# Reordering the end of the edge sweep in a graph-network and mixture-of-experts kernel

## The reference

```python
# x (3125, 256), 53125 edges (src, dst, type), sorted by dst, 8 relations, 16 experts, hidden 512
h_all = jnp.einsum('ni,roi->rno', layernorm(x), weight)       # 8 relations
msgs = h_all[edge_types, src]
x = x + jax.ops.segment_sum(msgs, dst, num_segments=3125) + bias
xn = layernorm(x)
probs = softmax(xn @ gate_w + gate_b)
top_probs, top_idx = jax.lax.top_k(probs, 2)                  # then normalised to sum 1
hidden = silu(xn @ w1[e]) * (xn @ w2[e])                      # for each chosen expert e
x = x + sum over the two experts of top_prob * (hidden @ w3[e])
```

## Time and profile before

| | |
|---|---|
| median of 3 runs | 988.91 us (986.33 to 989.62) |
| the profiled execution | 995.36 us |
| its span, first to last instruction | 993.7 us |
| its mean granted TensorE clock | 0.886 |
| busy: TensorE, VectorE, ScalarE, POOL | 759.2, 509.3, 262.6, 664.6 us |

### The profile page before, as it was taken

The page is one execution under the profiler, slowest core; times in us unless marked ns, Lnnn a source line. Parts: engine busy times, 40 slices in busy tenths (PEclk is TensorE's granted clock), DMA queues, the critical chain, the costliest instruction groups (busy, mean ns, idle before and its releaser), DMA issues.

```text
span 993.7 us, 18212 instructions
## 1 busy us (share of the span) xinstructions
PE 759.2 (76%) x4527; PEld 637.0 (64%) x4528; DVE 509.3 (51%) x1473; ACT 262.6 (26%) x397; POOL 664.6 (67%) x621
## 2 busy tenths in 40 slices
PE   0456797877888788788787884356998999998981
PEld 0334686765767566676666674245887888887871
DVE  6776444546444545544544746847443343443475
ACT  4721212223121222212222221221322232232323
POOL 1077777777777777777777730354768767778775
PEclk9965898989889988898988897577999999999995
DMA  8534444445444333433334312265365665556457
GB/s 203 172 102 143 144 143 142 141 140 179 142 135 129 105 105 104 128 105 106 106 111 120 106 54 87 92 202 202 116 202 173 201 196 174 184 192 215 132 154 219
DMA packets 93343, 144.16 MB, mean 145 GB/s; under 512 B 13335, under 2 KB 67563, under 8 KB 93322
## 3 DMA queue, kind: packets, MB, share of 16 engines
q0 software_dynamic: 25968, 70.94, 24.9%
q1 hardware_dynamic: 49856, 57.31, 18.0%
q10 hardware_dynamic: 17498, 15.68, 4.9%
HBM read 109.90 MB, written 33.98 MB: 145 GB/s over the span
## 4 chain that ended last, share of the span: by engine, by line
PE 44%; DMA 15%; issue 13%; POOL 10%; DVE 9%; DVEq 3%; ACT 3%; SPq 1%; ACTq 1%; POOLq 0%
PE ps L1383 15%; PE ps L1522 11%; PE ps L1373 8%; POOL got L521 7%; PE ps L1504 7%; DMA got<-x_tab,idx 6%; DMA y_tab<-ffn 4%; PE ps L1530 2%; DMA acc<-in_x 2%; ACT store L676 1%; POOL x_sb L557 1%; DVE store L958 1%; PE ps L1413 1%; DVE hot L940 1%; DVEq L958 1%
## 5 line engine op out<-in xcount | busy, mean ns | idle before, releaser
L521 POOL DMA_INDIRECT got<-x_tab,idx x425 | 405.2, 953 | 172.7 <-issue 155.3
L1373 PE MATMUL ps<-hot,got 125*128 125x256 f16 x1700 | 236.8, 302 | 108.3 <-DMA got<-x_tab,idx 96.0
L1373 PEld LDWEIGHTS ps<-hot,got 125*128 125x128 f16 x1700 | 177.1, 107 | 163.2 <-issue 115.7
L958 DVE TENSOR_TENSOR store<-store,ps 128x512 f32 x150 | 102.6, 684 | 233.9 <-PE ps L1373 209.7
L1383 PE MATMUL ps<-part,store 128*128 128x256 f32 x800 | 190.3, 398 | 0.0
L1522 PE MATMUL ps<-part,operands 128*128 x696 | 182.8, 413 | 5.6 <-POOL part L546 4.4
L1383 PEld LDWEIGHTS ps<-part,store 128*128 128x128 f32 x800 | 159.6, 203 | 22.4
L1522 PEld LDWEIGHTS ps<-part,operands 128*128 128x128 f32 x696 | 131.5, 196 | 34.0 <-issue 6.5
L940 DVE TENSOR_SCALAR hot<-key_row,pass,drel 125x256 f16<-125x256 f16 x425 | 124.8, 361 | 10.0 <-issue 9.9
L1504 PE MATMUL ps<-part,operands 128*128 x696 | 101.4, 296 | 18.9 <-DVE operands L1248 18.9
L1504 PEld LDWEIGHTS ps<-part,operands 128*128 128x128 f32 x696 | 90.1, 195 | 21.4 <-issue 21.4
(11 more groups left out here) (225 smaller groups left out, 584.0 us busy)
## 6 DMA issues: line engine op xcount, KB each, us to landing
store<-in_L_ffn_w SPq DMA_DIRECT2D x48, 512.0 KB, 5.9
xs_tab<-x_sb SPq DMA_DIRECT2D x16, 512.0 KB, 3.4
y_tab<-ffn SPq DMA_DIRECT2D x9, 896.0 KB, 4.5
ffn<-xs_tab ACTq DMA_DIRECT2D x59, 128.0 KB, 2.5
y_tab<-ffn ACTq DMA_DIRECT2D x58, 128.0 KB
got<-x_tab,idx POOLq DMA_INDIRECT x425, 2.7
acc<-in_x SPq DMA_DIRECT2D x5, 560.0 KB
x_tab<-got SPq DMA_DIRECT2D x5, 560.0 KB
```

Source lines behind the costliest of these rows:

```text
L521: nc.gpsimd.indirect_dma_start(got[:, c, :], None, x_tab, bass.IndirectOffsetOnAxis(ap=idx[:, c:c + 1], axis=0)).then_inc(gathered[c], 16)
L958: v.tensor_tensor(window, window, ps[:, WIN_BANK[g], :].rearrange("p (q n) -> p q n", n=WIN), ALU.add).then_inc(win_added, 1)
L1373: last = mm(ps[:, WIN_BANK[g], k * KEYS:(k + 1) * KEYS], got[0:CE, c, a * DIM + k * P:a * DIM + (k + 1) * P], hot[0:CE, g % HOT, c - c0, : ...
```

## The change

The sums of tile 24's groups 4 and 5 come directly behind group 3 on TensorE, ahead of the ranks and of tile 23's messages. The messages of tile 24 follow those of tile 23, with tile 23's transposes between its two halves. VectorE's additions of the three groups come ahead of `lanes` for the first 21 tiles. The one-hots of the lane are dealt out anew: 12 tiles after tile 23's normalisation, then 1 and 5 tiles around tile 24's, 3 tiles before the wait for the late ranks, and the last 4 at the end (before: 4, 6, 1 and 5 tiles, then 2 ahead of `code_row` and 7 at the end). On SP, expert 1's weights are loaded after tile 23's messages and expert 0's after tile 24's, and the last batch of `x2_tab` follows them. On ScalarE both `first_weights` come right after the sweep, expert 1's first.

```diff
@@ SP @@
-            for n in range(X_LOADS):
+            def store_x2(n):
...
+            for n in range(X_LOADS - 1):
+                store_x2(n)
             sp.wait_ge(tail_clear, visits + 1)
             sp.sem_inc(tiles_begun, 1)
+            sp.wait_ge(tile_summed, visits)
+            sp.sem_inc(tiles_begun, 1)
+            load_expert(0, 1, 1)
             sp.wait_ge(tile_summed, visits + 1)
             sp.sem_inc(tiles_begun, 1)
-            for k in range(2):
-                load_expert(0, k, k)
+            load_expert(0, 0, 0)
+            store_x2(X_LOADS - 1)
@@ ScalarE @@
+            first_weights(1)
+            first_weights(0)
             act.wait_ge(shift_done, 1)
...
-            first_weights(0)
             nc.scalar.activation(dev2[0:TP, :], mv2[0:TP, 1:2], ACT.Silu).then_inc(silu_loaded, 1)
...
             high_xs(0, 0)
-            first_weights(1)
             act.wait_ge(pos_done, 1)
@@ VectorE, turn() @@
-                    if at == 0 and last:
-                        dve.wait_ge(ranks_begun, b * GEN_W + w + 1)
-                        dve.sem_inc(stats2_begun, 1)
-                        lanes(0, FIRST_PART, then)
-                    elif at == 0 and then:
+                    if at == 0 and then and not last:
                         dve.wait_ge(tabs_zeroed, tab_stores * 16)
                         choose(0, 0, FIRST_PART, then)
                     if at == 0 and parts:
                         buffer_moved(v0 + i)
                     add_window(v0, t, g, w, i, second if at < HALF else first)
-                    if at == 0 and last:
-                        add_tile(n, node_tile(i - 1, b, single))
...
+                    if at == len(groups) - 1 and last:
+                        dve.wait_ge(ranks_begun, b * GEN_W + w + 1)
+                        dve.sem_inc(stats2_begun, 1)
+                        lanes(0, FIRST_PART, then)
+                        add_tile(n, node_tile(i - 1, b, single))
@@ VectorE, after the sweep's turns @@
                     normalize2(n - 1, tile)
-                    low_hots(0, 4)
+                    low_hots(0, 12)
                     add_gate_bias(n - 1, tile)
-                    low_hots(4, 10)
                     add_tile(n, tile_24, WIN_BANK[NG - 1])
-                    low_hots(10, 11)
+                    low_hots(12, 13)
                     normalize2(n, tile_24)
-                    low_hots(11, 16)
+                    low_hots(13, 18)
                     add_gate_bias(n, tile_24)
...
             v.tensor_tensor(top[:, 1, :], top[:, 1, :], top[:, 0, :], ALU.subtract).then_inc(shift_done, 1)
+            low_hots(18, FIRST_PART)
             dve.wait_ge(ranks_done, 1)
...
             lanes(FIRST_PART, TILES, step)
-            low_hots(16, 18)
             dve.wait_ge(code_spread, 1)
...
-            low_hots(18, TILES).then_inc(inv_hots, 1)
+            low_hots(FIRST_PART, TILES).then_inc(inv_hots, 1)
...
             def split_first(k, which):
-                dve.wait_ge(first_high, k + 1)
+                dve.wait_ge(first_high, 2)
@@ TensorE @@
-            def messages(n, at, groups, bank=MSG_BANK):
+            def messages(n, at, groups, bank=MSG_BANK, between=None):
...
                 for k in range(KT):
+                    if k == 1 and between is not None:
+                        turn_x2(between)
...
                     window(v0, t, 3)
+                    window(v0, t, 4)
+                    window(v0, t, 5)
...
                     ranks(0, FIRST_PART).then_inc(ranks_begun, 1)
                     turn_x2(v0 + t - 2)
                     messages(v0 + t - 1, 1, (v0 + t) * NG + HALF)
                     gate_logits(v0 + t - 2)
-                    window(v0, t, 4)
-                    window(v0, t, 5)
-                    turn_x2(v0 + t - 1)
-                    messages(v0 + t, 0, (v0 + t + 1) * NG, WIN_BANK[NG - 1])
+                    messages(v0 + t, 0, (v0 + t + 1) * NG, WIN_BANK[NG - 1], between=v0 + t - 1)
                     gate_logits(v0 + t - 1)
                     turn_x2(v0 + t)
                     gate_logits(v0 + t)
```

More of the change, by code:

```diff
@@ L708, in _, with first_weights @@
                     act.sem_inc(moved_on, 1)
+            def first_weights(k):
+                act.wait_ge(raw_in[k], 48)
+                nc.scalar.copy(part[:, 2 * k, :], raw[:, k, :]).then_inc(first_high, 1)
+            first_weights(1)
+            first_weights(0)
             act.wait_ge(shift_done, 1)
@@ L715, in _ @@
             nc.scalar.copy(upto_tile[:, FIRST_PART - 1:, :], late_at[0:1, :, :]).then_inc(upto_kept, 1)
-            def first_weights(k):
-                act.wait_ge(raw_in[k], 48)
-                nc.scalar.copy(part[:, 2 * k, :], raw[:, k, :]).then_inc(first_high, 1)
-            first_weights(0)
             nc.scalar.activation(dev2[0:TP, :], mv2[0:TP, 1:2], ACT.Silu).then_inc(silu_loaded, 1)
```

## The result

The changed kernel takes 976.6 us (median of 4 runs, 971.22 to 982.3) against 988.11 us of the kernel before. The ratio is 0.9891, with a 95% interval of 0.9861 to 0.9921. A second measurement, on one chip with four kernels, gave 975.07 against 987.39 us, ratio 0.9882 (0.9857 to 0.9908). The medians differ by 11.5 and 12.3 us, and the ratios give 10.8 and 11.7 us, where 6.9 were forecast. 976.6 lies 0.2 us inside the stated range, at the time of rival (a), to which the prediction gave 0.15; the second median, 975.07, lies outside the range.

A forecast was written before the change was run, and what follows sets the result against it. A chain of short waits ending at `first_idx` and `token` was taken to bound the start of the expert phase. Terms summed to -6.27 there, -6.87 after the early copy: 988.91 - 6.9 = 982.0 us, range 976.4 to 986.0.

The forecast's parts named there:

- rival (a): The escape: VectorE's eight small operations finish before POOL's split; fourth tile's operands 10.7 to 14.3 us earlier, 976.4; chance 0.15.
- The sums ahead of the ranks: TensorE: 20 sums put first make tile 23's multiplies end 2.22 us later; bounds +0.9 and +2.6.
- Tile 24's messages, additions, lanes: Tile 24's multiplies end at 605.65, 1.50 us earlier; VectorE's additions and `lanes` are not on the path.
- One-hots: VectorE: 24 take 5.5 us, covered with 0.4 to spare; with the later ones, -6.27 us in sum at `first_idx`.
- SP: Reordered weight loads and last rows on SP's queue: 20 us of room, so nothing taken.
- the early copy: ScalarE: first Silu 9.0 us earlier, but the extra 2.75 lost as POOL's split blocks VectorE's small operations; -6.87 inherited.
- 10.6 as the sign: TensorE's idle us in 250 us of expert phase; much more or less would show the forecast wrong.
- Rival (c): Gain given back in the expert phase, stores waiting behind weight loads, 2.6 us a time: 984.6 to 987.2; chance 0.12.
- (d): Slower: first result and weights collide through seven expert pairs, four more waits of 2.6 us, 992.4; chance 0.06.

The follow-up runs named there:

- the first four experiments: Changed kernel again, 0.9882; changed kernel with expert 1's weights copied late, 0.9969; kernel before with only that copy early, 0.9966; with only TensorE's and VectorE's part, 0.9953.

## Why the forecast was right in its sign, and short by 5 us

**The sums ahead of the ranks.** Forecast +2.22 at the end of tile 23's messages. Measured, long gap against long and short against short, +1.80 to +2.77, so the forecast was right in size; only the upper bound, +2.6, was a little low. What it missed is that the gap varies in both orders (1.44 and 2.53 us in the old, 0.64 to 3.10 in the new), and that its one profile of before was one with a long gap. The Trainium skill (Runtime: NRT & Kernel Launch, Instruction fetch mechanics) has the crossing of a block of code mostly hidden, and a stall behind a taken branch out of the blocks held. The three short gaps agree with the first; whether the loop's exit is a branch of the second kind no run shows.

**Tile 24's messages, additions, lanes.** As forecast: 0.23 us to the accumulation, 0.44 long, next messages 0.13 us later, the transposes in the middle without a wait. The end is 1.07 us earlier in the first profile (1.50 forecast); most of the difference is that of the step above. Tile 24's accumulation came 3.52 us earlier, where the forecast has 4.26 in its sum; its own times, 610.42 and 606.25, give 4.17.

**One-hots.** 5.44 us for 24 (5.5 forecast), covered with 0.78 us to spare. From tile 24's accumulation to `first_idx` it is 22.82 us against 24.76, -1.94 where +0.29 - 0.92 - 1.38 = -2.01 was forecast; `counts` lost 0.28 (0.29 forecast). `first_idx` came 5.46 us earlier, of 6.27.

**SP.** The last rows landed at 613.21, and the first gather of them started at 629.09: nothing, as forecast.

**The step that failed is the early copy.** The forecast said that its 2.75 us are "soon taken back", since two or three of the small operations get through and the rest wait for the end of POOL's split; 0.6 us would be left. Both profiles of the changed kernel, and that of the early copy alone, show rival (a)'s outcome in its place: in the changed kernel the second result's copy comes 31.8 and 32.0 us behind `first_idx`, not at the 33.2 worked out, and the split at 33.8 and 34.8, where 34.1 was worked out. Eight and nine of the nine operations (the forecast counted eight) get through unhindered. Two things made the copy earlier than forecast: the first result's store was landed and the copy begun 6.27 and 6.85 us after its issue (7.08 before), and the first Silu came 3.8 us earlier behind `first_idx`, not 2.75, as the stored rows landed faster (3.19 us against 4.05 in the chains). Rival (a) had expected the first of these to be 2 us; it is 0.8 and 0.2 us. Price of the late copy: 6.1 to 7.1 us at the fourth tile's operands (49.87 against 42.75 and 43.74), 9.0 us in the time, for 2.75 us of copy. Rival (a)'s 10.7 to 14.3 us, counted at those operands, came out as 14.1 in the first profile from the start of the 36 sums (15.2 from the first instruction). So it was not the forecast's own working that put 976.6 inside the range, but the range's reach to rival (a).

**The expert phase.** TensorE was busy 242.66 of 250 us from just after those operands on, against 239.43:

```profile
sum 250.00, PE 242.66 PEld 212.00 DVE 106.06 ACT 73.66 POOL 191.55; mean PE 242.66 PEld 212.00 DVE 106.06 ACT 73.66 POOL 191.55
```

TensorE so idled 7.3 us, where the forecast named 10.6 as the sign, and rivals (c) and (d) did not happen. But the profiles of the first four experiments, with late or early copy, have 240.19 to 242.20, so this gain of 3 us belongs to the one profile of before more than to the change. Rival (c) also read the 10.6 idle us too simply: 6.2 of them ended with VectorE's operands, and 4.4 with POOL's split.

**What stays open.** How often the kernel before is blocked in executions that are not profiled: by positions the early copy alone gains 7.1 us at the fourth tile, by time 3.4 (0.9 to 5.8). How the whole change does on the two slower chips, where the collision came back in spite of the early copy. And why those two chips take 21% longer with instructions of the same length.

## What to carry to other kernels

When another engine's long instruction can hold up an engine's small operations, a shift is worth more or less than itself: ask which side of the long instruction they fall on, and by how much. Here 1 us decided over 6 to 7. Moving such operations into a stretch in which the other engine doesn't compute does not hang on that 1 us: the third tile's operands stood at 36.8 to 38.3 us in all five profiles with them early, and at 34.0 to 42.3 in the others. Whether a loop's end is worth moving to where the engine has slack was not shown. And look at more than one profile of the kernel before: this forecast rested on one that was slower than all its other executions on such a chip.

## What was unexpected of the hardware

- VectorE's small operations with all operands in SBUF are held up by POOL's TENSOR_SCALAR too, not only by its TENSOR_TENSOR: 2.19 us and then 4.21 us for two of 125x25 elements that take 0.17 and 0.18 alone. One of them slips in between POOL's two instructions, which stand 0.08 us apart. A reciprocal in the same place took its usual 0.32, and so did an operation that reads PSUM (`operands`, 0.69 us at 664.33 under the split's second part). Which path the two engines share the traces do not show.
- The same 16 KB fetch at the end of TensorE's loop stood in a gap of 3.10 us in one execution and, coming 2 us sooner against the sums, left nothing beyond a gather's wait of 0.64 in another.
- The same kernel took 987 us on one chip and 1196 us on two others, with a window addition of VectorE at 684 and 687 ns.
